# Probabilities placed by head pair, and the product with the values in three fp32r matmuls, in a four-layer kernel

## The chip, the cores and the metric

The kernel runs on one NeuronCore of a Trainium2 chip as one program. The metric is the device time of one execution in microseconds (us), taken as the median over several runs. The engines are TensorE (PE in the profile; PEld is its weight load), VectorE (DVE), ScalarE (ACT), GpSimd (POOL) and SyncE (SP), which here only issues DMAs. Each works through its own instructions in order, and they wait for one another on semaphores.

## The reference

x has shape 8 x 128 x 512. Three low-rank or selected linear layers are added to it one after the other, and then an attention layer, in which this change lies:

```python
q, k, v = x @ Wq.T, x @ Wk.T, x @ Wv.T            # 32 query heads, 8 key/value heads, D = 128
q, k = rope(rmsnorm(q, q_norm_w), pos), rope(rmsnorm(k, k_norm_w), pos)
k_all = concat([k_cache[block_table], k])          # 512 cached positions + 128 new ones
v_all = concat([v_cache[block_table], v])
scores = einsum("bqhd,bkhd->bhqk", q, repeat(k_all, 4)) * SCALE
scores = where(valid, scores, -1e30)
probs = softmax(scores)                            # per head 128 queries x 640 keys
o = einsum("bhqk,bkhd->bqhd", probs, repeat(v_all, 4))
x = x + o.reshape(8, 128, 4096) @ Wo.T
```

All data are 32-bit floats.

## The kernel before

**Stages.** The first 120 us do the first three layers. Then come 64 units, one for each pair of key/value head and batch entry: a unit is one key/value head with its group of four query heads (GROUP), over 640 keys in five chunks of 128 (CH = 5, of which CCH = 4 are cached).

**One unit.** TensorE projects queries, key and value from x_s, turns the cached keys and the rotated queries, and computes the scores of the four heads into ps_s. VectorE adds the mask and takes the minimum (`lowest`), ScalarE takes the exponential (`exps`), VectorE the reciprocal of its sum (`inverse`), ScalarE multiplies by it (`normalize`). For the product with the values the probabilities must have the keys on the partitions: VectorE transposes 32 x 32 blocks (`turn_blocks`, line 1152), and the blocks are brought to their places by two DMAs through memory: `place_blocks` writes `blocks` to `blocks_dram` in four DMAs (line 364), waits for them, and reads it back into `prob_t` (line 371). Then `values` on TensorE multiplies: for each of two pairs of heads five chunks, stationary operand `v_raw` (cached) or `v_new`, moving operand 256 columns of `prob_t`, both plain 32-bit floats, which the chip does in two passes per matmul (20 rows for ten matmuls in the trace). The result is split into a rounded part and a remainder (`out_high` on ScalarE, `out_low` on VectorE) and multiplied by the output weights (`put_out`).

**Split products.** All other large products run in fp32r, a 32-bit format with rounded operands. Both operands are split into a rounded part and a remainder, and `three` does three matmuls: high x high, high x low, low x high. The helpers are `copy` (line 638) on ScalarE, `rest` (line 1055) on VectorE, and `weight_low` (line 106) on GpSimd.

**Order.** It is written out by hand as one function `step(n)` for each engine, in loops over n. Step n does the scores and probabilities of unit n, the projections and turned keys of unit n+1, the values of unit n-1 and the output product of unit n-2. On TensorE the order is: scores of pair 0, queries, scores of pair 1, key and value, turned cached keys, `put_out`, turned queries, `values(n-1)`. On GpSimd it is: copy of the new value into `v_new`, gather of the next values by an indirect DMA (line 493), remainder of a chunk of weights (line 106), sum of the rotated queries (line 509), norm factors `rstd` (line 513), gather of the next keys. ScalarE needs `rstd` to scale the new key (line 659), and TensorE needs that scaled key and the summed queries before it turns them (lines 876 to 880).

**Buffers.** `ps_o1` holds the turned cached keys and then the values product of pair 1, which waits for `kc_lo_out`, the remainder of those keys. Weights come in chunks until unit 54; from unit 55 on neither VectorE nor GpSimd splits weights.

## Time and profile before

| | us |
|---|---|
| median of three runs | 1224.59 |
| lowest and highest | 1222.09, 1231.84 |
| the profiled execution | 1230.89 |
| its span, first to last instruction | 1229.2 |
| TensorE busy | 1139.0 (93%) |
| VectorE busy | 850.5 (69%) |
| ScalarE busy | 683.5 (56%) |
| GpSimd busy | 475.6 (39%) |
| mean granted clock of TensorE | 0.985 of full |

The busy time of an engine is its instructions' time on one execution; instructions overlap a little, so sums of durations are somewhat above it. In a timeline row the first number is the start, the second the time until the last instruction of the row ended, and the bracket the idle time of the engine before it with what released it. The rows below use line numbers of the kernel before.

### The profile page before, as it was taken

Reading aid. Unit: us, or ns where it says so; the run is one execution under the profiler, and the core shown is the slowest. Engines: PE = TensorE matmul, PEld = TensorE weight load, DVE = VectorE, ACT = ScalarE, POOL = GpSimd, SP = SyncE. Lnnn points to the kernel's source line nnn. Section 1 sums busy time; section 2 is a strip of 40 time slices with the busy share of each in tenths; the row PEclk is TensorE's granted clock in tenths of the full one; section 3 lists DMA queues with packets and bytes.
Section 4 is the critical chain, followed back from the end, with each engine's and each line's share of the span. In section 5 each row is a group of like instructions: output and inputs, shape, how many; then the busy total and the mean of one; then the engine's idle time right before and its main releaser. Section 6 shows DMA issues by size and latency. Waiting matters only on the chain.

```text
span 1229.2 us, 27100 instructions
## 1 busy us (share of the span) xinstructions
PE 1139.0 (93%) x6112; PEld 979.4 (80%) x6112; DVE 850.5 (69%) x2167; ACT 683.5 (56%) x1914; POOL 475.6 (39%) x570
## 2 busy tenths in 40 slices
PE   5998789999999999999999999999999999999986
PEld 3555678888888888888888888888888888888874
DVE  2335667777777777777777777776777777777671
ACT  2223556665565665565666565665656665566550
POOL 6752334444333343333444333343333443232310
PEclk8999799999999999999999999999999999999998
DMA  5573477777777787777777777787777777767764
GB/s 171 189 273 133 136 229 231 241 236 226 238 242 242 245 252 230 228 247 240 240 239 227 233 249 238 241 255 229 218 243 237 249 226 221 233 215 227 241 197 137
DMA packets 83690, 277.31 MB, mean 226 GB/s; under 512 B 12633, under 2 KB 12761, under 8 KB 74459
## 3 DMA queue, kind: packets, MB, share of 16 engines
q1 hardware_dynamic: 71368, 236.23, 61.3%
q0 software_dynamic: 11152, 36.72, 10.1%
q10 hardware_dynamic: 1154, 4.19, 0.9%
q8 instruction: 6, 0.10, 0.0%
q14 instruction: 10, 0.07, 0.0%
HBM read 186.92 MB, written 90.18 MB: 225 GB/s over the span
## 4 chain that ended last, share of the span: by engine, by line
PE 50%; DMA 30%; DVE 7%; issue 6%; SPq 5%; ACT 1%; DVEq 0%; POOL 0%; POOLq 0%; ACTq 0%
DMA blocks_placed<-blocks 15%; DMA prob_t<-blocks_placed 13%; PE ps_o L911 12%; PE ps_q L848 8%; SPq L364 4%; PE ps_kv L848 4%; DVE blocks L1152 3%; PE ps_s L748 3%; PE ps_s L750 3%; PE ps_s L749 3%; PE ps_x L750 2%; PE ps_x L748 2%; DVE kt_lo L1055 2%; PE ps_x L749 2%; PE ps_l L780 2%
## 5 line engine op out<-in xcount | busy, mean ns | idle before, releaser
L911 PE MATMUL ps_o<-prob_t,v_raw 128*128 128x256 f32 x1024 | 251.5, 390 | 57.9 <-DMA prob_t<-blocks_placed 53.6
L685 ACT ACTIVATE prob<-prob,low 128x640 f32<-128x640 f32 x256 | 210.1, 825 | 126.8 <-DVE low L1134 117.3
L911 PEld LDWEIGHTS ps_o<-prob_t,v_raw 128*128 128x128 f32 x1024 | 193.9, 194 | 90.5 <-issue 60.5
L1134 DVE CUSTOM_DVE_ANT_0 prob<-ps_s,mask,q_gain 128x640 f32<-128x640 f32 x256 | 215.7, 880 | 35.6 <-PE ps_s L750 35.6
L1152 DVE STREAM_TRANSPOSE blocks<-prob 128x640 f32<-128x640 f32 x256 | 214.0, 837 | 0.4 <-ACT prob L690 0.2
L690 ACT ACTIVATE prob<-prob,inv 128x640 f32<-128x640 f32 x256 | 196.7, 817 | 0.6 <-DVE inv L1140 0.6
L638 ACT ACTIVATE ot_hi<-ps_o 128x256 fp32r<-128x256 f32 x128 | 49.2, 384 | 241.3 <-PE ps_o L911 241.3
L748 PE MATMUL ps_s<-kt_hi,qt_hi 128*128 (+2 forms) x512 | 172.0, 336 | 5.2 <-DVE kt_lo L1055 3.7
L848 PE MATMUL ps_q<-w_hi,x_s 128*128 (+1 forms) x512 | 172.6, 397 | 0.0
L750 PE MATMUL ps_s<-kt_hi,qt_lo 128*128 (+2 forms) x512 | 160.3, 313 | 0.0
L749 PE MATMUL ps_s<-kt_lo,qt_hi 128*128 (+2 forms) x512 | 160.0, 313 | 0.0
L520 POOL COPY v_new<-v_next 128x128 f32 (+1 forms) x64 | 18.5, 289 | 343.5 <-PE ps_o L911 335.2
L106 POOL TENSOR_TENSOR w_lo<-w_raw,w_hi 128x640 f32 (+1 forms) x64 | 100.6, 1572 | 98.0 <-DVE w_hi L100 96.7
L1055 DVE TENSOR_TENSOR ot_lo<-ps_o,ot_hi 128x256 fp32r<-128x256 f32 x128 | 53.1, 415 | 123.2 <-ACT ot_hi L638 123.2
L509 POOL TENSOR_TENSOR rot<-rot_a,rot_b 128x512 f32<-128x512 f32 x64 | 83.2, 1301 | 90.1 <-DVE rot_b L1081 90.1
L848 PEld LDWEIGHTS ps_q<-w_hi,x_s 128*128 128x128 f32 x512 | 96.8, 189 | 21.1
L748 PE MATMUL ps_x<-w_hi,ot_hi 128*128 (+1 forms) x256 | 106.3, 415 | 2.0 <-DVE ot_lo L1055 2.0
L748 PEld LDWEIGHTS ps_s<-kt_hi,qt_hi 128*128 128x128 f32 x512 | 97.4, 190 | 10.7 <-DVE kt_lo L1055 4.3
L513 POOL TENSOR_TENSOR rstd<-var,neg_half 128x5 f32<-128x5 f32 x64 | 77.2, 1206 | 70.2 <-DVE var L1089 70.2
L848 PE MATMUL ps_q<-w_lo,x_s 128*128 (+1 forms) x256 | 101.6, 397 | 0.0
L749 PEld LDWEIGHTS ps_s<-kt_lo,qt_hi 128*128 128x128 f32 x512 | 97.5, 190 | 4.6
L848 PE MATMUL ps_kv<-w_hi,x_s 128*128 (+1 forms) x512 | 100.9, 281 | 0.0
(138 smaller groups left out, 2212.0 us busy)
## 6 DMA issues: line engine op xcount, KB each, us to landing
blocks_placed<-blocks SPq DMA_DIRECT2D x256, 320.0 KB
prob_t<-blocks_placed SPq DMA_DIRECT2D x64, 1280.0 KB
x_s<-xt_split SPq DMA_DIRECT2D x64, 512.0 KB
w_raw<-w_qkvo_dram SPq DMA_DIRECT2D x55, 320.0 KB
w<-w_t_dram SPq DMA_DIRECT2D x8, 1024.0 KB, 5.8
xt_split<-x3t ACTq DMA_DIRECT2D x8, 512.0 KB
w_raw<-w_qkvo_dram POOLq DMA_DIRECT2D x9, 320.0 KB, 5.7
xbt<-x_t_dram SPq DMA_DIRECT2D x8, 256.0 KB, 2.7
```

The costliest lines, as they stand in the source:

```text
L106: return nc.gpsimd.tensor_tensor(lo, raw, hi.bitcast(F32), ALU.subtract)
L509: nc.gpsimd.tensor_tensor(rot[:, 0:GROUP, :], rot_a[:, 0:GROUP, :], rot_b[:, 0:GROUP, :], ALU.add).then_inc(q_summed, 1)
L685: nc.scalar.activation(prob[:, h, :], prob[:, h, :], ACT.Exp, bias=low[:, h:h + 1], scale=-1.0, accum_out=total[:, h:h + 1]).then_inc(exp_ ...
L690: nc.scalar.activation(prob[:, h, :], prob[:, h, :], ACT.Copy, scale=inv[:, h:h + 1]).then_inc(prob_done, 1)
L748: nc.tensor.matmul(dst, lh, rh, start=first, stop=False)
L749: nc.tensor.matmul(dst, lh, rl, start=False, stop=False)
L750: return nc.tensor.matmul(dst, ll, rh, start=False, stop=final)
L848: mm = nc.tensor.matmul(dst, x_s[:, int(i % 3 == 2), k * P:(k + 1) * P], w_rest if i % 3 == 1 else w, start=i == 0, stop=i == 3 * KT - 1)
L911: mm = nc.tensor.matmul(ps_o[pair][:, 0:PAIR], v, turned_probs(c, pair), start=c == 0, stop=c == CH - 1)
L1055: return nc.vector.tensor_tensor(dst, src, high.bitcast(F32), ALU.subtract)
L1134: nc.vector.tensor_tensor_reduce(out=prob[:, h, :], in0=ps_s[:, score_slot(h):score_slot(h) + KEYS], in1=mask[:, :], scale=q_gain[:, h:h + ...
L1152: nc.vector.transpose(blocks[:, :, :, h, :].rearrange("p j c q -> p c j q"), prob[:, h, :].rearrange("p (c j k) -> p c j k", c=CH, j=NB)). ...
```

## The change

The placing of the probabilities is cut in two: `place_blocks(n, pair)` writes and reads back one pair of heads, with its own part of `blocks_dram`, `prob_t` and semaphores, and starts as soon as that pair is turned. A unit then has eight writes, each of 32 x 4 pieces of 1280 bytes (before, four with pieces of 2560 bytes), and two reads of 640 KB.

The product with the values goes through `three`. For this both operands are split. The values: VectorE rounds the 640 columns of `v_raw` (which now holds the new value too) into `v_hi` (`values_high`), GpSimd takes the remainder `v_lo` (`values_low`). The probabilities: ScalarE rounds each pair, 1280 columns, into `pt_hi` (`probs_high`), and VectorE and GpSimd each subtract over half of the columns (640), in place in `prob_t` (`probs_low_first`, `probs_low_rest`). `values` waits for both halves of each pair. Since `v_raw` is free once it is split, the gather of the next values waits for `v_split`, and it is issued one unit earlier.

```diff
-        blocks_dram = nc.dram_tensor("blocks_placed", [NB, BLOCK, NB, CH * GROUP * BLOCK], F32).ap()
+        blocks_dram = nc.dram_tensor("blocks_placed", [2, NB, BLOCK, NB, RUN], F32).ap()
...
-            v_new = sb("v_new", [P, D], scope=p2)
             prob = sb("prob", [P, GROUP, KEYS], scope=p2)
-            blocks = sb("blocks", [P, NB, CH, GROUP, BLOCK], scope=p2)
-            prob_t = sb("prob_t", [P, NB * CH * GROUP * BLOCK], scope=p2)
+            blocks = sb("blocks", [P, 2, NB, CH, GROUP // 2, BLOCK], scope=p2)
+            prob_t = sb("prob_t", [P, 2, NB * RUN], F32R, scope=p2)
+            pt_hi = sb("pt_hi", [P, 2, NB * RUN], F32R, scope=p2)
+            v_hi = sb("v_hi", [P, CH * D], F32R, scope=p2)
+            v_lo = sb("v_lo", [P, CH * D], F32R, scope=p2)
...
+            CUT = NB // 2 * RUN
...
-                    def place_blocks(n, first=False):
-
-                        sp.wait_ge(blocks_turned, GROUP * (n + 1))
+                    def place_blocks(n, pair, first=False):
+
+                        sp.wait_ge(blocks_turned, GROUP * n + 2 * pair + 2)
                         sp.nop(nofuse=True)
                         if not first:
-                            sp.wait_ge(pt_in, 16 * n)
+                            sp.wait_ge(pt_in[pair], 16 * n)
                             sp.nop(nofuse=True)
                         for a in range(NB):
-                            sp.dma_start(blocks_dram[:, :, a, :].rearrange("j i r -> i j r"),
-                                         blocks[a * BLOCK:(a + 1) * BLOCK, :, :, :, :].rearrange("p j c h q -> p j (c h q)")).then_inc(blocks_out, 16)
-                        sp.wait_ge(blocks_out, 16 * NB * (n + 1))
+                            sp.dma_start(blocks_dram[pair, :, :, a, :].rearrange("j i r -> i j r"),
+                                         blocks[a * BLOCK:(a + 1) * BLOCK, pair, :, :, :, :].rearrange("p j c h q -> p j (c h q)")).then_inc(blocks_out[pair], 16)
+                        sp.wait_ge(blocks_out[pair], 16 * NB * (n + 1))
                         sp.nop(nofuse=True)
                         if not first:
-                            sp.wait_ge(pv_done, 2 * n)
+                            sp.wait_ge(pv_done, 2 * (n - 1) + pair + 1)
                             sp.nop(nofuse=True)
-                        sp.dma_start(prob_t[:, :], blocks_dram.rearrange("j i a r -> (j i) (a r)")).then_inc(pt_in, 16)
+                        sp.dma_start(prob_t[:, pair, :].bitcast(F32), blocks_dram[pair].rearrange("j i a r -> (j i) (a r)")).then_inc(pt_in[pair], 16)
...
-                        place_blocks(n, first)
+                        place_blocks(n, 0, first)
+                        place_blocks(n, 1, first)
...
-                        pool.wait_ge(pv_done, 2 * u)
+                        pool.wait_ge(v_split, u)
...
-                    def move_new_value(u, values):
+                    def move_new_value(u, first=False):
+                        if not first:
+                            pool.wait_ge(v_split, u)
+                            pool.nop(nofuse=True)
                         pool.wait_ge(vn_out, u + 1)
-                        if values:
-                            pool.wait_ge(pv_done, 2 * u)
                         pool.nop(nofuse=True)
-                        nc.gpsimd.tensor_copy(v_new[:, :], next_value(u)).then_inc(vn_moved, 1)
-
-                    def step(n, weights, keys, last, first=False, second=False):
-
-                        if not first:
-                            move_new_value(n - 1, not second)
-                            if not second:
-                                next_values(n - 1)
+                        nc.gpsimd.tensor_copy(v_raw[:, CCH * D:], next_value(u)).then_inc(vn_moved, 1)
+
+                    def values_low(u):
+                        pool.wait_ge(v_hi_out, u + 1)
+                        nc.gpsimd.tensor_tensor(v_lo[:, :], v_raw[:, :], v_hi[:, :].bitcast(F32), ALU.subtract).then_inc(v_split, 1)
+
+                    def probs_low_rest(u, pair):
+                        pool.wait_ge(pt_hi_out, 2 * u + pair + 1)
+                        nc.gpsimd.tensor_tensor(prob_t[:, pair, CUT:], prob_t[:, pair, CUT:].bitcast(F32),
+                                                pt_hi[:, pair, CUT:].bitcast(F32), ALU.subtract).then_inc(pt_lo_rest, 1)
+
+                    def step(n, weights, keys, last, first=False):
+
+                        if not first:
+                            values_low(n - 1)
+                        move_new_value(n, first)
+                        if not first:
+                            next_values(n)
                         if weights:
                             pool.wait_ge(w_rounded, n + AHEAD + 1)
                             weight_low(n + AHEAD, w_raw[:, 0, :]).then_inc(w_split, 1)
+                        if not first:
+                            probs_low_rest(n - 1, 0)
                         if not last:
                             sum_queries(n + 1)
                             norm_factors(n + 1)
+                        if not first:
+                            probs_low_rest(n - 1, 1)
...
+                    def probs_high(u, pair):
+                        act.wait_ge(pt_in[pair], 16 * (u + 1))
+                        copy(pt_hi[:, pair, :], prob_t[:, pair, :].bitcast(F32)).then_inc(pt_hi_out, 1)
+
                     def step(n, last, head=True, out=True, first=False):
                         if head:
                             out_high(n - 2, 1, first=first)
                         exps(n, 0)
                         exps(n, 1)
+                        if out:
+                            probs_high(n - 1, 0)
                         normalize(n, 0)
...
+                            probs_high(n - 1, 1)
                         normalize(n, 2)
...
-                        pe.wait_ge(v_in, 16 * (u + 1))
-                        pe.wait_ge(vn_moved, u + 1)
-                        pe.wait_ge(pt_in, 16 * (u + 1))
+                        pe.wait_ge(v_split, u + 1)
                         if not first:
                             pe.wait_ge(ot_lo_out, 2 * u)
                         for pair in (0, 1):
+                            pe.wait_ge(pt_lo_first, 2 * u + pair + 1)
+                            pe.wait_ge(pt_lo_rest, 2 * u + pair + 1)
                             if pair == 1:
                                 pe.wait_ge(kc_lo_out, cached)
                             for c in range(CH):
-                                v = v_raw[:, c * D:(c + 1) * D] if c < CCH else v_new[:, :]
-                                mm = nc.tensor.matmul(ps_o[pair][:, 0:PAIR], v, turned_probs(c, pair),
-                                                      start=c == 0, stop=c == CH - 1)
+                                cut = slice(c * D, (c + 1) * D)
+                                mm = three(ps_o[pair][:, 0:PAIR], (v_hi[:, cut], v_lo[:, cut]),
+                                           (turned_probs(pt_hi, c, pair), turned_probs(prob_t, c, pair)), c == 0, c == CH - 1)
                             mm.then_inc(pv_done, 1)
...
+                    def values_high(u, first=False):
+                        dve.wait_ge(v_in, 16 * (u + 1))
+                        dve.wait_ge(vn_moved, u + 1)
+                        dve.wait_ge(xt_stored, 16 * B) if first else dve.wait_ge(pv_done, 2 * u)
+                        nc.vector.tensor_copy(v_hi[:, :], v_raw[:, :]).then_inc(v_hi_out, 1)
+
+                    def probs_low_first(u, pair):
+                        dve.wait_ge(pt_hi_out, 2 * u + pair + 1)
+                        rest(prob_t[:, pair, 0:CUT], prob_t[:, pair, 0:CUT].bitcast(F32), pt_hi[:, pair, 0:CUT]).then_inc(pt_lo_first, 1)
...
+                        if out:
+                            values_high(n - 1, first=not head)
                         dve.wait_ge(mask_set, n + 1)
...
                         turn_blocks(n, 1)
+                        if out:
+                            probs_low_first(n - 1, 0)
                         inverse(n, 2)
...
                             cached_low(n + 1, ps_o1)
-                        turn_blocks(n, 2)
+                        if out:
+                            probs_low_first(n - 1, 1)
+                        turn_blocks(n, 2, first)
```

On GpSimd the next-to-last step (unit 62, written out without the loop's register rows; in the loop the remainder of the weights, `w_lo`, stands between the gather and `rot`) reads before:

```order
L520 COPY v_new<-v_next 128x128
L490 COPY v_row<-row_id 128x1
L493 DMA v_raw<-v_rows_dram,v_row 128x512
L509 TENSOR_TENSOR rot<-rot_a,rot_b 128x512
L513 TENSOR_TENSOR rstd<-var,neg_half 128x5
```

and now:

```order
L533 TENSOR_TENSOR v_lo<-v_raw,v_hi 128x640
L529 COPY v_raw<-v_next 128x128
L498 COPY v_row<-row_id 128x1
L501 DMA v_raw<-v_rows_dram,v_row 128x512
L537 TENSOR_TENSOR prob_t<-prob_t,pt_hi 128x640
L517 TENSOR_TENSOR rot<-rot_a,rot_b 128x512
L521 TENSOR_TENSOR rstd<-var,neg_half 128x5
L537 TENSOR_TENSOR prob_t<-prob_t,pt_hi 128x640
```

Two remainders stand ahead of the norm factors `rstd` that did not stand there, and one behind them.

On ScalarE, in the loop, from the scaling of the new key to the rounding of the turned queries and key, before:

```order
L659 ACTIVATE rot<-key_sum,rstd 128x128
L638 ISA
L638 ACTIVATE kt_hi<-ps_o 128x512
L690 ACTIVATE prob<-prob,inv 128x640 x2
L638 ACTIVATE qt_hi<-ps_q 128x512
L638 ISA
L638 ACTIVATE kt_hi<-ps_kv 128x128
```

and now:

```order
L682 ACTIVATE rot<-key_sum,rstd 128x128
L661 ISA
L661 ACTIVATE kt_hi<-ps_o 128x512
L661 ACTIVATE pt_hi<-prob_t 128x1280
L713 ACTIVATE prob<-prob,inv 128x640 x2
L661 ACTIVATE qt_hi<-ps_q 128x512
L661 ISA
L661 ACTIVATE kt_hi<-ps_kv 128x128
```

The rounding of pair 1 stands behind the cached keys and ahead of the last two normalizations.

On VectorE, in the loop, from the remainder of the cached keys to the last transposed head, before:

```order
L1055 TENSOR_TENSOR kt_lo<-ps_o,kt_hi 128x512
L1152 STREAM_TRANSPOSE blocks<-prob 128x5x4x32
L1055 TENSOR_TENSOR qt_lo<-ps_q,qt_hi 128x512
L1055 ISA
L1055 TENSOR_TENSOR kt_lo<-ps_kv,kt_hi 128x128
L1106 TENSOR_SCALAR q_gain<-rstd 128x4
L1152 STREAM_TRANSPOSE blocks<-prob 128x5x4x32
```

and now (line 1088 is `rest`):

```order
L1088 TENSOR_TENSOR kt_lo<-ps_o,kt_hi 128x512
L1187 REGISTER_ALU
L1088 TENSOR_TENSOR prob_t<-prob_t,pt_hi 128x640
L1195 STREAM_TRANSPOSE blocks<-prob 128x5x4x32
L1088 TENSOR_TENSOR qt_lo<-ps_q,qt_hi 128x512
L1088 ISA
L1088 TENSOR_TENSOR kt_lo<-ps_kv,kt_hi 128x128
L1139 TENSOR_SCALAR q_gain<-rstd 128x4
L1195 STREAM_TRANSPOSE blocks<-prob 128x5x4x32
```

VectorE's half of pair 1 stands ahead of the third transposed head.

## Rows read from the trace of the kernel before

**Rows 1.** The page's first part: busy time, share of the span, instructions

```profile
PE 1139.0 (93%) x6112; PEld 979.4 (80%) x6112; DVE 850.5 (69%) x2167; ACT 683.5 (56%) x1914; POOL 475.6 (39%) x570
```

**Rows 2.** Waits, grouped: us in total, times, longest

```profile
PE ps_o L911 <- DMA prob_t<-blocks_placed: 53.6, 32, 3.1
```

**Rows 3.** Timeline of PE, 610 to 646 us: start, us, what [idle before <-releaser]

```profile
611.12 1.97 PE L911 MATMUL ps_o<-prob_t,v_raw 128*128 128x256 f32 x8 [1.57 <-DMA prob_t<-blocks_placed]
...
627.03 1.89 PE L911 MATMUL ps_o<-prob_t,v_raw 128*128 128x256 f32 x8
...
631.16 0.47 PE L748 MATMUL ps_s<-kt_hi,qt_hi 128*128 x1
...
644.69 1.53 PE L911 MATMUL ps_o<-prob_t,v_raw 128*128 128x256 f32 x6 [1.64 <-DMA prob_t<-blocks_placed]
```

**Rows 4.** The chain that ended last, 600 to 680 us: start, us, what

```profile
622.02 1.42 PE ps_kv L848 x12
...
632.58 6.19 DMA blocks_placed<-blocks
638.96 5.46 DMA prob_t<-blocks_placed
```

**Rows 5.** Timeline of DVE, 628 to 646 us

```profile
629.66 0.83 DVE L1152 STREAM_TRANSPOSE blocks<-prob 128x640 f32<-128x640 f32 x1
...
631.96 0.42 DVE L1055 TENSOR_TENSOR ot_lo<-ps_o,ot_hi 128x256 fp32r<-128x256 f32 x1 [0.77 <-ACT ot_hi L638]
...
634.52 0.49 DVE L100 CAST w_hi<-w_raw 128x640 f32 x1
...
643.34 0.68 DVE L1055 TENSOR_TENSOR kt_lo<-ps_o,kt_hi 128x512 f32 x1
```

**Rows 6.** Timeline of SyncE's queue, 628 to 662 us

```profile
630.70 3.45 SPq L364 DMA_DIRECT2D blocks_placed<-blocks  x4
```

**Rows 7.** Timeline of POOL, 631 to 645 us, one step

```profile
631.80 0.29 POOL L520 COPY v_new<-v_next 128x128 f32 x1 [4.26 <-PE ps_o L911]
632.04 0.18 POOL L490 COPY v_row<-row_id 128x1 int32 x1
633.00 0.97 POOL L493 DMA_INDIRECT v_raw<-v_rows_dram,v_row  x1 [0.77 <-POOL v_row L490]
635.56 1.58 POOL L106 TENSOR_TENSOR w_lo<-w_raw,w_hi 128x640 f32 x1 [1.59 <-DVE w_hi L100]
637.84 1.30 POOL L509 TENSOR_TENSOR rot<-rot_a,rot_b 128x512 f32<-128x512 f32 x1 [0.70 <-DVE rot_b L1081]
640.21 1.21 POOL L513 TENSOR_TENSOR rstd<-var,neg_half 128x5 f32<-128x5 f32 x1 [1.07 <-DVE var L1089]
```

**Rows 8.** Timeline of ACT, the same step

```profile
631.55 0.38 ACT L638 ACTIVATE ot_hi<-ps_o 128x256 fp32r<-128x256 f32 x1 [1.77 <-PE ps_o L911]
...
635.48 1.54 ACT L690 ACTIVATE prob<-prob,inv 128x640 f32<-128x640 f32 x2
...
641.51 0.41 ACT L659 ACTIVATE rot<-key_sum,rstd 128x128 f32<-128x128 f32 x1
641.82 0.58 ACT L638 ACTIVATE kt_hi<-ps_o 128x512 f32 x1
```

**Rows 9.** Timeline of POOL and DVE in the first stage, 62 to 90 us

```profile
63.70 0.69 DVE L970 TENSOR_TENSOR xbt_lo<-xbt,xbt_hi 128x512 fp32r<-128x512 f32 x1 [4.89 <-ACT xbt_hi L555]
...
86.87 1.53 POOL L106 TENSOR_TENSOR w_lo<-w_raw,w_hi 128x640 fp32r<-128x640 f32 x1
...
87.29 1.67 DVE L970 TENSOR_TENSOR xbt_lo<-xbt,xbt_hi 128x512 fp32r<-128x512 f32 x1 [4.89 <-ACT xbt_hi L555]
```

**Rows 10.** Timeline of PE, 838 to 858 us

```profile
845.90 2.65 PE L911 MATMUL ps_o<-prob_t,v_raw 128*128 128x256 f32 x8 [1.92 <-DMA prob_t<-blocks_placed]
```

**Rows 11.** Windows: busy time of each engine, PE's granted clock, DMA share

```profile
848.00:850.00 2.00, 2.00 (x6) 1.58 (x5) 0.15 (x1) 0.39 (x1) 0.00 (x0) 0.50 0.83 181
```

**Rows 12.** Timeline of PE at the end

```profile
1215.70 3.65 PE L911 MATMUL ps_o<-prob_t,v_raw 128*128 128x256 f32 x8 [4.27 <-DMA v_raw<-v_rows_dram,v_row]
```

35 lines of the change are left out of this document (22 added, 13 removed).

## The prediction

> **What bounds the kernel now.** First the share of the engines: TensorE is busy 93% of the span [rows 1]. That suggests a TensorE bound, but the waits show the one thing it still waits for in the steady state: in 32 units, every second one, the values product waits for the probabilities to come back from memory, 53.6 us in all [rows 2]. TensorE's timeline shows the rhythm: the product starts at 611.12, 627.03 and 644.69 [rows 3]. One unit takes 15.91 us without the wait, the next 17.66 with it, so two take 33.57 and one 16.79. The chain over the same stretch tells which loop that is [rows 4]: the last head of unit n is turned (629.66 plus 0.83, so 630.49 [rows 5]), SyncE issues four writes (630.70, 3.45 us [rows 6]), they have landed by 638.77, the read is issued at 638.96 and takes 5.46, and TensorE starts at 644.69 [rows 3, 4]. From the turned head to the product it is 14.2 us, and the product of the unit before stands ahead of the scores from which the next probabilities are made. So the kernel runs on a loop over two units, with pure TensorE work (15.9 a unit) close under it.
>
> **TensorE's part.** A unit has 20 passes of 256 columns; those up to 631.16 began at 627.03, so they take 4.13 us, or 0.21 each [rows 3]. An fp32r matmul of 256 columns takes 0.118: 12 of them 1.42 [rows 4]. The change makes 30, that is 3.55 us. TensorE's work falls by 0.6 to 15.3 a unit. The moving operand keeps its pattern of runs of 32 columns; fp32r with such runs is not in the trace. The value taken is 0.118, from the same number of columns; the other end is the 0.21 of the plain passes with the same runs, which would make 6.2 us and 2.7 more a unit.
>
> **The placing.** By pair, the leg from the last turned head to its data shrinks. Before: 8.3 to the landed writes, 0.2, 5.7 to TensorE [rows 3 to 6]. A pair has as many write pieces as the whole had, of half the size, and half the read. If issuing sets the pace (3.45 for the same count of pieces) and a tail of about 2 stays, a write takes 5.6 and a read about 3.8, 9.5 together. The upper bound is that nothing shrinks: 14.2 for each pair. Pair 0 starts after the second head. From its end to the last head's, VectorE has two more heads of 0.83, three operations on 512 columns of about 0.68 and some small ones, some 4.2 us by [rows 5], and now two halves of 0.8 in between. The last head is turned 0.7 before the product ends (630.49 against 631.16 [rows 3, 5]), now up to a microsecond later, so pair 1's data is there 9 to 10 us into the next step. ScalarE comes to it after the cached keys, 11 us in (641.82 against 631.16 [rows 3, 8]). Pair 0's data comes some 6 us before pair 1's, 3 to 4 us in, and ScalarE comes to it after two exponentials, 4.3 us in (635.48 [rows 8]). So the placing is hidden, by about 1 us for either pair. This loop is gone as the bound, and the question is what is late next.
>
> **What is late next: GpSimd.** The order gives GpSimd three more subtractions of 640 columns per step, each as long as the one of weights, 1.58 us [rows 7], 4.7 us together. In the gaps of 39% busy [rows 1] they would fit. But they lie in one chain that closes over a single unit, because rounding the values has to wait for the product of the unit before (it overwrites what that reads), and GpSimd's norm factors stand behind everything it does with values, weights and pair 0. I follow it from the last matmul of the product through one step, with the row for each piece:
>
> - ScalarE's `ot_hi` starts 0.05 later, VectorE's `ot_lo` 0.41 after it [rows 5, 8], `v_hi` 0.35 after that and takes 0.49, as the cast of 640 columns does [rows 5]. Sum 1.30.
> - GpSimd, 0.1 later: `v_lo` 1.58, 0.1, the new value 0.24, from the row copy to the gather 0.96, the gather 0.97, weights 1.58, pair 0's remainder 1.58, `rot` 1.30, `rstd` 1.21 [rows 7]. Sum 10.92. In the row of before `rstd` was done at 641.42, 9.9 after the product, since it had idle time ahead of each piece.
> - ScalarE: 0.09, the new key 0.31 (641.51 to 641.82), the cached keys 0.58 less 0.1 of overlap [rows 8], then rounding pair 1. Its price: from 256 to 512 columns 0.38 becomes 0.58, so 768 more cost 0.6, in all 1.2; two operations of 640 take 1.54 [rows 8]. I take 1.25. Sum 13.05.
> - GpSimd's half of pair 1: 0.05, 1.58, 0.1. Sum 14.78.
> - TensorE: 15 matmuls 1.77, and 0.16 until the last has ended. **Sum 16.71 us.**
>
> That is already the 16.79 of before. Two places can only add.
>
> **The two halves of a remainder** wait for the same `pt_hi`, and both engines are free by then (VectorE's `cached_low` ends as the rounding does). VectorE's half costs 0.81: 0.42 for 256 columns, 0.68 for 512 [rows 5]. Whether the two run beside each other is the disputed cost. The rows of the first stage show the same pair of instructions meeting: GpSimd subtracts from 86.87 to 88.40, VectorE's subtraction of two SBUF operands starts at 87.29 and takes 1.67 instead of 0.69 (63.70), that is until 0.56 after GpSimd's end [rows 9]. So one waits for the other. Whoever is first, the pair of halves takes 2.13 (GpSimd first) to 2.33 (VectorE first), not 1.58: plus 0.55 to 0.75. I take 0.75: VectorE starts 0.41 after ScalarE does [rows 5, 8], that is at once, GpSimd some 0.1 later. The other place is the copies of `v_hi` and of the weights on VectorE, which fall beside GpSimd's small copies: 0 to 0.5, I take 0.3.
>
> The Trainium skill says the same in "SBUF — State Buffer", section "SBUF: two separate sides": VectorE and GpSimd share one port pair under an exclusive lock, taken also by a VectorE instruction with two SBUF inputs against a GpSimd one that reads SBUF. By this rule splitting a remainder between the two engines is little better than doing the halves in turn; the trace agrees in the one meeting above, and without the lock the sum would stay at 16.71.
>
> So a step takes 16.71 + 0.75 + 0.3 = 17.76 us, 0.97 more than before. **Steps without weights** (the last eight or so) lose 1.58 on GpSimd: about 16.2, 0.6 less than before. **At the end** the product waited for the gather of the values (4.27 us, until 1215.70 [rows 12]), which is now issued a unit earlier, and the last leg shrinks from 14.2 + 4.1 to about 9.5 + 1.25 + 2.3 + 1.8: some 4 less, I take 5 with the gather. Sum: 53 x 0.97 - 8 x 0.6 - 5 = +42 us.
>
> The profiled execution took 1230.89, so it would be 1273. The median of before is 0.5% under its profiled execution: **1267 us**.
>
> **What hides the rest.** ScalarE's rounding of pair 0 (1.25) stands ahead of two normalizations; the squares behind them wait for VectorE's rotation (line 1081) and leave idle time, and behind the squares `rstd` is later than ScalarE in any case, so I count nothing; without that cover it would be 1.25 a step. VectorE gets 2.1 us more; 69% busy [rows 1] of 16.79 is 11.6, so at least 13.7 of 17.8. Its last turned head moves some 2 us later, which the placing can bear. If the GpSimd chain were shorter, TensorE would be next: 15.3 and, as an estimate, 0.5 of waits for the rounding of pair 1, 15.8.
>
> **Rivals.**
>
> *The halves run side by side* and the small copies cost nothing: 16.71 a step, 53 x -0.08 - 5 - 5 = -14, profiled 1217, so 1211 to 1225. For it: only one such meeting is shown. Against: that one [rows 9]. 13%.
>
> *Faster: the GpSimd chain doesn't close*, because its instructions overlap or the values part is finished before TensorE asks, and the two gains show: no wait on the placing, 0.6 less on TensorE. The next bound is 15.8 a step: 61 x -1.0 = -60, so 1165. It decides by the length of GpSimd's part: a gain of over 1% needs a step under 16.6, 1.2 less than my sum, so each of the three new subtractions would have to cost 0.4 less, or `rstd` to be done 9.7 us after the product. In the rows GpSimd's instructions follow each other without overlap [rows 7]. 10%.
>
> *The placing is the bound*: a write by pair takes as long as before. SyncE blocks on each: 2 x (8.3 + 0.3) + 0.9 for the two other issues is 18.1 us a step, and pair 0 comes too late for ScalarE. Then 18.2 to 18.7 a step, 61 x 1.65 = +100, so 1325. For it: the count of pieces is the same for half the bytes, and the issue alone is 3.45. Against: half the bytes. 12%.
>
> *TensorE's clock.* With the forecast it idles twice per step, about 1 us before the turned queries and 2 us before pair 1. In the steady part of before a single wait of 1.92 us [rows 10] was followed by a stretch at a granted clock of 0.50, which is the level of 1.2 GHz [rows 11], while those of 1.57 and 1.64 [rows 3] were not. Both matmul groups behind the waits are on the loop; if it fell in every second unit for 3.4 us, it would cost 0.9 a unit more: 1315. 10%.
>
> **How the numbers follow.** My forecast, 1250 to 1290, has 55%. The range of 8 in 10 leaves out the fast rival and the worst of the slow ones: 1212 to 1328. A measurement of this kernel can tell about 1% from no change. Faster by over 1% (under 1212): the fast rival and a part of the first, 14%. Within 1%: the rest of the first and the low edge of the forecast, 14%. Slower: 72%.
>
> **What would show it.** In the profile after: `rstd` some 10.9 us after the end of the values product, with GpSimd without idle time from `v_lo` to it; TensorE waiting for the scaled key before the turned queries (about 1 us) and for `pt_lo_rest` before pair 1 (1.5 to 2 us), in every unit and no longer in every second; the wait on `prob_t` gone from TensorE and not on ScalarE; one of the two halves of pair 1 at 1.4 us or more (VectorE) or 2.3 (GpSimd); fp32r passes 0.118 apart. Wrong would be: ScalarE's `pt_hi` waiting for a DMA, `pt_lo` halves overlapping at 0.81 and 1.58, or a clock under 0.95.

## The result, and the profile after

The changed kernel takes 1278.44 us, the median of four runs (1278.27 to 1279.61), the kernel before 1228.21 beside it: a ratio of 1.0415, 95% interval 1.0361 to 1.0469. **It is 4.2% slower.** The profiled execution took 1278.57 us, its span is 1276.9.

The page of the changed kernel, the parts on busy time and on the chain that ended last:

```profile
PE 1103.5 (86%) x6752; PEld 961.1 (75%) x6752; DVE 1045.5 (82%) x2359; ACT 816.8 (64%) x2042; POOL 813.0 (64%) x762
...
POOL 32%; PE 29%; issue 19%; DVE 8%; ACT 5%; POOLq 3%; DMA 2%; DVEq 1%; SPq 0%; ACTq 0%
```

Against [rows 1], TensorE has lost 35 us of busy time in spite of 640 more matmuls, and GpSimd has gained 337. The second line is the finding. In the kernel before it begins with PE 50% and DMA 30%. Now DMA has 2%, and GpSimd, the engine with the lowest busy share beside ScalarE, leads with 32%. An engine that is busy 64% of the time can be the bound if the rest is waiting inside its own loop.

The waits of the changed kernel, grouped (us in total, times, longest):

```profile
POOL prob_t L537 <- ACT pt_hi L661: 147.6, 66, 4.6
...
POOL v_lo L533 <- DVE v_hi L1184: 106.0, 63, 4.5
...
PE ps_o L781 <- issue: 80.5, 58, 4.3
...
ACT rot L682 <- POOL rstd L521: 78.4, 59, 1.9
PE ps_q L912 <- ACT rot L682: 56.4, 57, 2.3
```

The wait of TensorE for `prob_t` from memory [rows 2] isn't there any more. In its place stand five that hang together and come in nearly every unit. They form a loop: `v_hi`, `v_lo`, ..., `rstd`, `rot`, `pt_hi`, `prob_t`, the product.

One step on TensorE's timeline (the second pair's product starts at 601.98 and at 619.73, 17.75 us apart; in nearly all units with weights it is 17.7 to 17.8):

```profile
601.98 0.36 PE L781 MATMUL ps_o<-pt_hi,v_hi 128*128 128x256 f32 x1 [1.37 <-issue]
602.17 0.28 PE L782 MATMUL ps_o<-prob_t,v_hi 128*128 128x256 f32 x1
602.29 0.28 PE L783 MATMUL ps_o<-pt_hi,v_lo 128*128 128x256 f32 x1
...
615.87 0.63 PE L912 MATMUL ps_q<-ident,rot 128*128 128x128 f32 x4 [0.92 <-ACT rot L682]
...
619.73 0.36 PE L781 MATMUL ps_o<-pt_hi,v_hi 128*128 128x256 f32 x1 [1.36 <-issue]
```

GpSimd's timeline between the two:

```profile
605.35 1.57 POOL L533 TENSOR_TENSOR v_lo<-v_raw,v_hi 128x640 fp32r<-128x640 f32 x1 [1.51 <-DVE v_hi L1184]
607.33 0.29 POOL L529 COPY v_raw<-v_next 128x128 f32 x1 [0.40 <-POOL v_lo L533]
...
608.54 0.99 POOL L501 DMA_INDIRECT v_raw<-v_rows_dram,v_row  x1 [0.77 <-POOL v_row L498]
609.54 1.59 POOL L107 TENSOR_TENSOR w_lo<-w_raw,w_hi 128x640 f32 x1
611.07 1.58 POOL L537 TENSOR_TENSOR prob_t<-prob_t,pt_hi 128x640 fp32r<-128x640 f32 x1
612.59 1.31 POOL L517 TENSOR_TENSOR rot<-rot_a,rot_b 128x512 f32<-128x512 f32 x1
614.02 1.21 POOL L521 TENSOR_TENSOR rstd<-var,neg_half 128x5 f32<-128x5 f32 x1
617.45 2.18 POOL L537 TENSOR_TENSOR prob_t<-prob_t,pt_hi 128x640 fp32r<-128x640 f32 x1 [2.22 <-ACT pt_hi L661]
```

ScalarE's in the same step:

```profile
604.02 0.39 ACT L661 ACTIVATE ot_hi<-ps_o 128x256 fp32r<-128x256 f32 x1 [2.04 <-PE ps_o L783]
...
615.32 0.40 ACT L682 ACTIVATE rot<-key_sum,rstd 128x128 f32<-128x128 f32 x1 [1.40 <-POOL rstd L521]
615.63 0.58 ACT L661 ACTIVATE kt_hi<-ps_o 128x512 f32 x1
616.11 1.26 ACT L661 ACTIVATE pt_hi<-prob_t 128x1280 fp32r<-128x1280 f32 x1
```

And VectorE's:

```profile
604.78 0.48 DVE L1184 CAST v_hi<-v_raw 128x640 fp32r<-128x640 f32 x1
...
612.41 1.53 DVE L1122 TENSOR_SCALAR var<-sq 128x5 f32<-128x5 f32 x1
...
617.41 0.81 DVE L1088 TENSOR_TENSOR prob_t<-prob_t,pt_hi 128x640 fp32r<-128x640 f32 x1
```

Read in order of time this is the chain: product ends, `ot_hi` 604.02, `v_hi` 604.78, `v_lo` 605.35, every piece on GpSimd close behind the one before until 615.23, `rot` 615.32, `pt_hi` 616.11 to 617.37, GpSimd's half 617.45 to 619.63, product 619.73. In [rows 7] GpSimd waits 1.59, 0.70 and 1.07 us ahead of three of these pieces. Here those waits are gone. The last half takes 2.18 us instead of 1.58, because VectorE began its own half 0.04 earlier.

SyncE's queue in the same step:

```profile
612.04 0.35 SPq L356 DMA_DIRECT2D x_s<-xt_split  x1
612.72 0.34 SPq L361 DMA_DIRECT2D w_raw<-w_qkvo_dram  x1
615.67 1.83 SPq L371 DMA_DIRECT2D blocks_placed<-blocks  x4
619.92 0.34 SPq L378 DMA_DIRECT2D prob_t<-blocks_placed  x1
621.33 2.33 SPq L371 DMA_DIRECT2D blocks_placed<-blocks  x4
626.98 0.34 SPq L378 DMA_DIRECT2D prob_t<-blocks_placed  x1
```

Four writes are issued and have landed 4.25 us later for pair 0 and 5.65 for pair 1. For all heads at once it was 8.3 [rows 4, 6].

### The profile page after: what moved, and what is told of

It reads as the page before. It is cut to its first block, busy times and chain, and to the rows that moved or that the text cites. A ratio compares the mean times of both kernels' runs of the same rounds, so it can differ in the third digit from the quotient of the medians.

```text
span 1276.9 us, 30220 instructions
## 1 busy us (share of the span) xinstructions
PE 1103.5 (86%) x6752; PEld 961.1 (75%) x6752; DVE 1045.5 (82%) x2359; ACT 816.8 (64%) x2042; POOL 813.0 (64%) x762
## 4 chain that ended last, share of the span: by engine, by line
POOL 32%; PE 29%; issue 19%; DVE 8%; ACT 5%; POOLq 3%; DMA 2%; DVEq 1%; SPq 0%; ACTq 0%
POOL v_lo L533 7%; POOL w_lo L107 7%; POOL prob_t L537 7%; PE ps_o L781 6%; POOL rot L517 6%; POOL rstd L521 5%; PE ps_o L783 5%; PE ps_o L782 5%; PE ps_q L912 3%; PE ps_l L813 2%; DVE v_hi L1184 2%; ACT rot L682 2%; ACT ot_hi L661 2%; DVE blocks L1195 1%; DVE prob_t L1088 1%
## 5 line engine op out<-in xcount | busy, mean ns | idle before, releaser
L537 POOL TENSOR_TENSOR prob_t<-prob_t,pt_hi 128x640 fp32r<-128x640 f32 x128 | 237.8, 1858 | 147.8 <-ACT pt_hi L661 147.6
L781 PE MATMUL ps_o<-pt_hi,v_hi 128*128 128x256 f32 x640 | 191.5, 299 | 91.6 <-issue 80.5
L781 PEld LDWEIGHTS ps_o<-pt_hi,v_hi 128*128 128x128 f32 x640 | 121.0, 189 | 104.1 <-issue 95.7
L782 PE MATMUL ps_o<-prob_t,v_hi 128*128 128x256 f32 x640 | 181.7, 284 | 0.0
L783 PE MATMUL ps_o<-pt_hi,v_lo 128*128 128x256 f32 x640 | 181.2, 283 | 0.0
L533 POOL TENSOR_TENSOR v_lo<-v_raw,v_hi 128x640 fp32r<-128x640 f32 x64 | 100.9, 1577 | 106.0 <-DVE v_hi L1184 106.0
L661 ACT ACTIVATE pt_hi<-prob_t 128x1280 fp32r<-128x1280 f32 x128 | 161.3, 1260 | 10.3 <-DMA prob_t<-blocks_placed 10.3
L782 PEld LDWEIGHTS ps_o<-prob_t,v_hi 128*128 128x128 f32 x640 | 121.4, 190 | 0.0
L783 PEld LDWEIGHTS ps_o<-pt_hi,v_lo 128*128 128x128 f32 x640 | 121.1, 189 | 0.0
L1088 DVE TENSOR_TENSOR prob_t<-prob_t,pt_hi 128x640 fp32r<-128x640 f32 x128 | 109.5, 856 | 7.0 <-ACT pt_hi L661 7.0
```

The source lines that it names most:

```text
L533: nc.gpsimd.tensor_tensor(v_lo[:, :], v_raw[:, :], v_hi[:, :].bitcast(F32), ALU.subtract).then_inc(v_split, 1)
L537: nc.gpsimd.tensor_tensor(prob_t[:, pair, CUT:], prob_t[:, pair, CUT:].bitcast(F32), pt_hi[:, pair, CUT:].bitcast(F32), ALU.subtract).then ...
L661: return nc.scalar.activation(dst, src, ACT.Copy)
L781: nc.tensor.matmul(dst, lh, rh, start=first, stop=False)
L782: nc.tensor.matmul(dst, lh, rl, start=False, stop=False)
L783: return nc.tensor.matmul(dst, ll, rh, start=False, stop=final)
```

## The experiments

All times are medians, with the ratio to the kernel before, run on the same chip, and its 95% interval. "Step" is the mean distance between the first score operations (`low`) of two units on VectorE, units 8 to 52, when weights are still loaded. "Writes" is the mean time on SyncE from the first of four writes to the read behind them, for pair 0 and pair 1, between 200 and 1050 us. Runs 4, 6 and 7 leave work or bytes out and compute something else; they only show what a part costs.

| kernel | us | ratio | step | writes |
|---|---|---|---|---|
| before | 1224.7 to 1228.2 | 1 | 16.79 | 7.8, all heads |
| after | 1278.44 | 1.0415 | 17.79 | 4.25, 6.00 |
| 1 placing by pair alone | 1256.99 | 1.0292 (1.0225 to 1.0358) | 17.32 | 8.05, 6.28 |
| 2 pair 0's half late | 1219.85 | 0.9962 (0.9933 to 0.9992) | 16.70 | 4.56, 5.16 |
| 3 pair 1 on VectorE | 1258.47 | 1.0297 (1.0240 to 1.0353) | 17.44 | 5.81, 6.20 |
| 4 no remainders | 1239.52 | 1.0137 (1.0083 to 1.0192) | 17.07 | 6.03, 6.17 |
| 5 pair 0 on VectorE | 1220.14 | 0.9962 (0.9928 to 0.9997) | 16.71 | 4.51, 5.12 |
| 6 = 4, keys behind | 1199.73 | 0.9813 (0.9776 to 0.9850) | 16.31 | 5.04, 6.30 |
| 7 = 1, short inputs | 1162.89 | 0.9502 (0.9477 to 0.9528) | 15.86 | 5.65, 6.80 |
| 8 one placing | 1810.99 | 1.4794 (1.4752 to 1.4836) | 26.05 | 7.8, all heads |
| 9 = 1, ScalarE loads | 1213.76 | 0.9907 (0.9876 to 0.9937) | 16.62 | 7.18, 6.81 |
| 10 = before, ScalarE loads | 1233.25 | 1.0068 (1.0041 to 1.0095) | 16.84 | 7.7, all heads |
| 11 = 5, ScalarE loads | 1250.56 | 1.0217 (1.0171 to 1.0263) | 17.26 | 5.46, 5.70 |
| 12 = after, ScalarE loads | 1326.21 | 1.0820 (1.0778 to 1.0862) | 18.71 | 5.13, 6.55 |

### 1. Only the placing by pair

The kernel before with the placing of the changed one; the product stays f32.

```diff
-                        place_blocks(n, first)
+                        place_blocks(n, 0, first)
+                        place_blocks(n, 1, first)
```

> The kernel before with the placing by head pair alone; the product with the values stays in plain 32-bit floats, and nothing is split. Theory (the loop over two units through the placing was the bound before, and the pairs break it): the wait of 1.6 to 1.7 us in every second unit goes, and a unit takes TensorE's own 15.9 us instead of 16.8: some 54 us less, a ratio to before of 0.956, about 1175 us. Rival (SyncE, blocked on two writes in turn, takes the place of the loop, or the next wait is close behind): ratio 0.99 to 1.01.

Slower, 1.0292. The theory, that the placing is hidden once it is done by pair, failed. SyncE's queue in this kernel:

```profile
614.70 0.35 SPq L350 DMA_DIRECT2D x_s<-xt_split  x1
615.37 0.34 SPq L355 DMA_DIRECT2D w_raw<-w_qkvo_dram  x1
616.03 3.08 SPq L365 DMA_DIRECT2D blocks_placed<-blocks  x4
624.89 0.34 SPq L372 DMA_DIRECT2D prob_t<-blocks_placed  x1
625.46 2.26 SPq L365 DMA_DIRECT2D blocks_placed<-blocks  x4
631.25 0.34 SPq L372 DMA_DIRECT2D prob_t<-blocks_placed  x1
632.25 0.35 SPq L350 DMA_DIRECT2D x_s<-xt_split  x1
```

The loop over two units through the turned heads is indeed gone (SyncE waits for turned blocks 3.6 us in all), but it is replaced by SyncE's own round: issue the inputs, write, wait, read, write, wait, read, 17.55 us from `x_s` to `x_s`. SyncE waits 586.5 us for writes to land, and pair 0's writes, of half the bytes, take as long as those of the whole had (8.05 against 7.8).

### 2. GpSimd's half of pair 0 behind the norm factors

```diff
-                        if not first:
-                            probs_low_rest(n - 1, 0)
                         if not last:
                             sum_queries(n + 1)
                             norm_factors(n + 1)
                         if not first:
+                            probs_low_rest(n - 1, 0)
                             probs_low_rest(n - 1, 1)
```

> The changed kernel with one instruction moved: GpSimd's half of pair 0's remainder stands behind the norm factors instead of ahead of the sum of the queries. Theory (one chain through GpSimd closes over each step, and this piece of 1.58 us lies on it): a step falls from 17.75 us to VectorE's bound, seen in the steps without weights, of about 16.7: 53 x 1.05 = 56 us less, about 1222 us, ratio to before 0.995. Rival (the bound is the load of VectorE or the count of instructions of GpSimd, not their order): within 5 us of 1278, ratio 1.04.

As the theory had it. The same work in another order gives 1219.85 us, 58 less than the changed kernel, so the chain through `rstd` was the bound. In this kernel TensorE's one wait is for VectorE's half (0.84 and 0.21 us), and VectorE is busy 754 of the 800 us from 200 to 1000.

### 3. Pair 1's remainder wholly on VectorE

```diff
-                        if not first:
-                            probs_low_rest(n - 1, 1)
```

VectorE's subtraction goes over 1280 columns for pair 1.

> The changed kernel with the whole remainder of pair 1 on VectorE, 1280 columns in one instruction, and none of it on GpSimd; pair 0 as it is. Theory (the two halves exclude each other, so that the pair of them takes 2.25 us from the rounding): one instruction takes 1.49 us, a step 0.75 less, 53 x 0.75 = 40 us less, about 1239, ratio 1.009. Rival (the halves run side by side and the 2.19 us of GpSimd's half have another cause): 1.49 instead of 1.58, 5 us less, ratio 1.037. A second rival: VectorE is so full that its longer instruction gives back more than half: ratio 1.025 or more.

A miss for the theory: 1.0297, the step fell by only 0.35. It is the second rival, a full VectorE. The loop through GpSimd is still the one that closes. One turn of it:

```profile
604.70 1.48 DVE L1086 TENSOR_TENSOR prob_t<-prob_t,pt_hi 128x1280 fp32r<-128x1280 f32 x1
610.05 1.58 POOL L533 TENSOR_TENSOR v_lo<-v_raw,v_hi 128x640 fp32r<-128x640 f32 x1 [5.55 <-DVE v_hi L1182]
620.04 0.40 ACT L679 ACTIVATE rot<-key_sum,rstd 128x128 f32<-128x128 f32 x1 [0.60 <-POOL rstd L521]
```

From the end of the rounding to the end of the subtraction it is 1.53 us, 0.73 less than the 2.26 of the two halves. But VectorE then works without a gap from 604.70 until the end of `v_hi` at 609.96, and comes to `v_hi` later: 1.69 us from the product to its end instead of 1.28. From there to the end of `rstd` it is 9.99, ScalarE takes 2.13 and TensorE 2.09, in sum 17.43. The 5.55 us ahead of `v_lo` are GpSimd's wait for `v_hi`; they don't take it out of the loop. ScalarE's `pt_hi` also waits for the read now, 77.7 us in all, in 62 units. SyncE is not the bound: it waits for turned heads 160.1 us in all.

### 4. No remainders of the probabilities

```diff
-                            pe.wait_ge(pt_lo_first, 2 * u + pair + 1)
-                            pe.wait_ge(pt_lo_rest, 2 * u + pair + 1)
+                            pe.wait_ge(pt_hi_out, 2 * u + pair + 1)
```

The four subtractions of a unit are left out as well.

> The changed kernel without the four subtractions that take the remainder of the probabilities: the placed probabilities themselves are multiplied where the remainder was. Rounding, splitting of the values, placing and all 30 matmuls stay. Theory: the chain loses 1.58 for pair 0 and 2.25 for pair 1, and a step comes to TensorE's 15.3 plus some waits, 15.6: about 130 us less than the changed kernel, 1148 us, ratio 0.935. Rival (the values' part or the placing is a bound of its own): a step stays above 16.4, ratio 0.98 or more.

Again a miss: with all four halves gone, 1239.52 us. SyncE's queue:

```profile
614.38 0.34 SPq L361 DMA_DIRECT2D w_raw<-w_qkvo_dram  x1
617.01 2.39 SPq L371 DMA_DIRECT2D blocks_placed<-blocks  x4
623.30 0.34 SPq L378 DMA_DIRECT2D prob_t<-blocks_placed  x1
```

and ScalarE's rounding of the pair of the unit before:

```profile
610.79 1.27 ACT L655 ACTIVATE pt_hi<-prob_t 128x1280 fp32r<-128x1280 f32 x1 [1.80 <-DMA prob_t<-blocks_placed]
```

Pair 0's writes take 6.29 us, against 4.25 in the changed kernel, with the same bytes and pieces. Here a second loop has become the bound, and it isn't SyncE's queue, which waits for turned heads 134.1 us in all, in nearly every unit ahead of pair 0's writes (the 2.29 us between 614.72 and 617.01). It goes through the data of pair 0: writes, read, rounding (`pt_hi` waits for the read in 59 units, 85.2 us), normalizations, turned head, writes of the next unit, 17.07 us in the mean. Two things could stretch the writes. GpSimd's key gather is issued at 617.45 here, 0.4 us after them (at 620.54 in the changed kernel, when they have landed), and the transfers of `x_s` and `w_raw` are issued shortly ahead. Run 6 takes the first away here; run 7 takes the second away in run 1's kernel.

### 5. Pair 0's remainder wholly on VectorE

With no half of pair 0 left on GpSimd, this is the changed kernel with one assignment changed: VectorE subtracts over all 1280 columns of pair 0. Against run 2:

```diff
-                            probs_low_rest(n - 1, 0)
                             probs_low_rest(n - 1, 1)
```

> The kernel with GpSimd's half of pair 0 behind the norm factors, and that half now given to VectorE: VectorE subtracts the whole 128x1280 of pair 0, pair 1 stays in halves. Theory (two engines that meet over the same stretch gain nothing): in the kernel that it starts from VectorE's half of pair 0 lasts 2.06 us, because GpSimd's 1.55 us half is in its way, and TensorE waits 0.84 us for it; the whole remainder alone on VectorE should take about 1.5 us (cached_low does 512 columns from PSUM in 0.68, a half of 640 takes 0.8 when undisturbed), so the step falls from 16.7 to about 16.1 us and the time to 1190 (0.970 of the kernel before the change). Rival: the placing through SyncE is already nearly the bound (it set 17.3 us a step in the two runs whose VectorE or GpSimd was relieved), so a key gather that is issued earlier stretches pair 0's writes and the time stays at 1220 or rises to 1245.

The same time as run 2, so the theory's further 30 us didn't come. VectorE's timeline says why:

```profile
604.92 1.45 DVE L1086 TENSOR_TENSOR prob_t<-prob_t,pt_hi 128x1280 fp32r<-128x1280 f32 x1
607.61 1.61 DVE L1086 TENSOR_TENSOR prob_t<-prob_t,pt_hi 128x640 fp32r<-128x640 f32 x1
```

Pair 0 takes the 1.45 us expected, but now pair 1's half meets GpSimd's (606.97 to 608.54) and takes 1.61 instead of 1.01. In run 2 the two took 2.06 + 1.01 = 3.07 us of VectorE's time, here 1.45 + 1.61 = 3.06. The stall moved and didn't shrink. The rival named the number (1220), but its reason was wrong, since the writes took 4.51 us and TensorE waited for VectorE alone.

### 6. Run 4, with the key gather behind pair 0's writes

```diff
                         if keys:
+                            pool.wait_ge(blocks_out[0], 16 * NB * (n + 1))
                             next_keys(n + 2)
```

> The kernel without remainders of the probabilities (the placed probabilities themselves are multiplied where the remainder stood, so the sum is another), and GpSimd's gather of the cached keys now waits until pair 0's writes have landed. Theory (the key gather is in the writes' way): there the gather is issued 0.4 us after pair 0's writes and these take 6.3 us, against 4.25 to 4.5 us in the two kernels whose gather comes later; moved behind them the writes fall to about 4.5 us, the step from 17.4 to about 16.0 us, and the time from 1239.5 to about 1170 (0.955). Rival (the writes are slow because SyncE issues them within 2.6 us of the two input transfers, whoever gathers what): writes stay at 6 us or more, the step at 17.3 us, the time at 1235 to 1245 (1.01).

The writes of pair 0 fell from 6.03 to 5.04 us and the step from 17.07 to 16.31, so the gather's place does cost here. It is a good half of what the theory asked.

### 7. Run 1, with short input transfers

```diff
-                        sp.dma_start(x_s[:, :, :].bitcast(F32), xt_dram[bass.ds(u & 7, 1), :, :, :].rearrange("a p s c -> p (a s) c")).then_inc(x_s_in, 16)
+                        sp.dma_start(x_s[:, :, 0:64].bitcast(F32), xt_dram[bass.ds(u & 7, 1), :, :, 0:64].rearrange("a p s c -> p (a s) c")).then_inc(x_s_in, 16)
```

and `w_raw` the same.

> The kernel before the change with the placing by pair alone, and SyncE's transfers of the next input and weights cut from 512 and 320 KB to an eighth and a tenth (the rest of the tiles keeps old numbers, so the output is another). Theory (pair 0's writes stand in line behind these 832 KB, which SyncE issues 0.7 to 1.3 us ahead of them): pair 0's writes fall from 8.2 to 8.9 us to about 6 us, the step from 17.4 to about 16.0 us or to what TensorE's own work takes, and the time from 1257 to about 1175 to 1190 (0.965). Rival (the writes are limited by their own 1280-byte pieces and the gathers): pair 0's writes stay above 7.5 us, the time above 1240.

Better than the theory's number: 1162.89 us, and every step from the third unit on is 15.8 to 16.0 us. The window of the steady part, with each engine's busy time, PE's granted clock, DMA share and GB/s:

```profile
200.00:1000.00 800.00, 800.00 (x4487) 717.17 (x4486) 632.60 (x1663) 513.09 (x1458) 334.84 (x403) 1.00 0.68 205
```

TensorE is busy 800 us of 800. This is what [rows 3] called the 15.9 of pure TensorE work, and it is the floor of this kernel with the f32 product. Pair 0's writes fell from 8.05 to 5.65 us.

### 8. The changed kernel with one placing per unit

```diff
-                        place_blocks(n, 0, first)
-                        place_blocks(n, 1, first)
+                        place_blocks(n, first)
```

> The changed kernel with one placing per unit again, as before the change (2560-byte pieces, one read of 1280 KB), the three matmuls, the rounding and the halves all kept and in the same order. Theory (the new order of the engines needs pair 0's probabilities early): ScalarE rounds pair 0 some 4 us after the last head of the unit before has been turned, while the whole placing lands about 10 us after it, so ScalarE waits 5 to 6 us for it at every step, with everything behind it; the step grows to about 20 us or more and the time to 1380 to 1450 (1.15). Rival (GpSimd's chain alone sets 17.75 us and the wait lies in its shadow): the time stays at 1278 (1.04) or falls, since the wide pieces are written faster.

The sign as expected and the size far beyond: 1810.99, a step of 26.05 us. From its waits:

```profile
ACT pt_hi L663 <- DMA prob_t<-blocks_placed: 591.7, 64, 10.2
```

That is 9.2 us a unit, and it lies on the path, since ScalarE normalizes the next heads only behind `pt_hi`, and the next placing needs those. The step is 8.3 us longer. A part may be the clock, which the theory had left out: between 200 and 1000 us TensorE is busy 529.90 of 800 us and its mean granted clock is 0.83 of full, against 1.00 in the changed kernel. How much of the step that is, no run here shows apart. The two parts of the change can't be taken apart in this order: the product as written needs the placing by pair.

### 9 to 12. The input transfers issued by ScalarE

In four kernels `x_s` and `w_raw`, whole again, are issued by ScalarE: `x_s` behind the new value, `w_raw` between the scaled key and the cached keys.

```diff
+                        if weights:
+                            next_weights(n + 1)
                         if not last:
                             cached_high(n + 1, ps_o1, first=not out)
```

Run 9 is run 1 with it:

> The kernel before the change with the placing by pair alone, and the transfers of the next input and the next weights, whole again, issued by ScalarE on its own queue instead of by SyncE. Theory (pair 0's writes stand in line behind these 832 KB on SyncE's queue, and SyncE, which waits for each landing, is the loop): pair 0's writes fall from 8.2 to 8.9 us to 5.5 to 6.5 us, and SyncE saves the 1.3 us of two issues, so the step falls from 17.4 to 15.9 to 16.3 us and the time from 1257 to about 1165 to 1190 (0.96 of the kernel before). Rival (the transfers share the same DMA engines from whichever queue, and it is their bytes that cost): pair 0's writes stay at 7.5 us or more, SyncE gains only its issue time, and the time is 1225 to 1250 (1.01).

1213.76 us, between the two. Pair 0's writes fell by 0.9 us only, pair 1's rose by 0.5. SyncE also saves 1.3 us of issuing, and the step fell by 0.70; SyncE now waits for turned heads again, 73.9 us in all. So of the 2.4 us by which run 7 shortened pair 0's writes, most came from fewer bytes, not from a free queue, while of the 1.46 us of its step about half comes with all bytes kept. The Trainium skill has the rule in "DMA: Bandwidth & Descriptors", section "Issuing engines are not separate DMA queues": whoever issues, the transfers run on the same 16 DMA engines, and issuing from several saves the issue time only. Writes of 7.18 us against 5.65 agree with it.

Run 10 is the kernel before with it:

> The kernel before the change, unchanged but for the transfers of the next input and the next weights, which ScalarE issues. Theory (in the kernel before, SyncE waits for turned blocks after it has issued them, so they have landed before the writes start and nothing stands in line): the writes keep their 5.6 us, the loop of two units its 33.6 us, and the time is 1225 within 1% (1.00). Rival (the gain of the run with short inputs was simply fewer bytes in the chip, or a freer SyncE, and comes with any placing): 1195 or less (0.975).

As the theory had it, within 1%.

Run 11 is run 5 with it:

> The changed kernel with pair 0's remainder wholly on VectorE, and the two input transfers issued by ScalarE. Theory (there VectorE is the bound, TensorE waits for it alone, 0.25 and 0.79 us a step, and the writes, 4.4 us, are off the path): the time stays at 1220 (0.996 of the kernel before). Rival (the placing still holds a part of that step): 1195 (0.975).

Run 12 is the changed kernel with it:

> The changed kernel, unchanged but for the two input transfers, which ScalarE issues. Theory (GpSimd's chain closes over one step at 17.75 us and the placing lies in its shadow): the step stays at 17.7 to 17.8 us and the time at 1278 (1.042 of the kernel before). Rival (pair 1's placing, which ScalarE waits for in a few steps, or the key gather still sets part of the step): 1265 or less (1.03).

Both missed, and on the slow side. I hadn't counted that ScalarE's issue of `w_raw` stands between `rot` and `kt_hi`. In the changed kernel `kt_hi` begins 0.31 us after `rot`; in run 12 it is 0.84 (617.81 and 618.65). ScalarE is 64% busy, but these 0.53 us lie on the loop, and where the loop runs undisturbed the step is 18.3 us, 0.55 more than 17.75. The rest, up to the mean of 18.71, goes with the clock. TensorE's two waits in one unit of run 12, ahead of the turned queries and of pair 1's product:

```profile
806.12 0.63 PE L930 MATMUL ps_q<-ident,rot 128*128 128x128 f32 x4 [0.93 <-ACT rot L682]
810.53 0.36 PE L799 MATMUL ps_o<-pt_hi,v_hi 128*128 128x256 f32 x1 [1.88 <-issue]
```

and the window behind them (the clock is the third number from the end):

```profile
812.00:816.00 4.00, 4.00 (x20) 3.96 (x19) 2.06 (x5) 0.38 (x1) 1.95 (x2) 0.60 0.91 276
```

Behind waits of 0.93 and 1.88 us the granted clock fell to 0.60 of full in this window (a mixture of 2.4 and 1.2 GHz), and over 200 to 1000 us it was 0.96. The step that follows took 18.81 us. In the changed kernel the same two waits are 0.92 and 1.36 us, and the clock was 1.00. So run 12 shows what the rival on TensorE's clock had described, and the changed kernel doesn't.

In run 11 the same issue stands there (`kt_hi` begins 0.68 us after `rot`), but the loop is VectorE's. Its half of pair 1 now begins at 603.32, 0.09 us behind GpSimd's, and takes 2.15 us instead of the 1.61 of run 5, where it began 0.64 behind. That is the 0.55 us by which the step grew (16.71 to 17.26).

## Why the prediction was right, and where it was not

The sign, the mechanism and the step were right: 17.76 us forecast, 17.75 read. Not every term was.

| from the last product, us | forecast | after |
|---|---|---|
| to the end of `v_hi` | 1.30 | 1.28 |
| GpSimd to the end of `rstd` | 9.62 | 9.97 |
| ScalarE to the end of `pt_hi` | 2.13 | 2.14 |
| the two halves | 2.38 | 2.26 |
| TensorE, with 0.1 to its start | 2.03 | 2.10 |
| copies beside copies | 0.30 | 0 |
| sum | 17.76 | 17.75 |

- **GpSimd's part** lacked 0.35: 0.30 of it is the new value's copy, which begins 0.40 after `v_lo` and not 0.1.
- **The halves** do exclude each other, with VectorE first, as forecast. The pair took 2.26 and not 2.38.
- **The 0.3 for the copies** of `v_hi` and of the weights wasn't there (0.48 and 0.49, as alone). That the sum is right to 0.01 is luck. Its terms are right to 0.35.
- **fp32r** passes are 0.118 apart with runs of 32 columns as without, and TensorE does less work, as forecast. It buys nothing, since TensorE waits.
- **The placing is hidden** came true in the changed kernel (ScalarE waits for it 10.3 us in all). But the prediction gave it as a property of the placing by pair, and run 1 shows that it isn't: alone it makes the kernel 2.9% slower. The missing step is SyncE's round. With two placings it waits for two landings per unit, and the writes are issued beside 832 KB of inputs and a gather. I had priced that round at 18.1 us for the rival "the placing is the bound", and gave that rival 12%; in run 1 it closes at 17.3. In the changed kernel SyncE's queue has room, since it waits 203.8 us for turned heads. Nearer is the rival's other half, pair 0's data coming too late for ScalarE: that loop closes at 17.07 in run 4, with writes of 6.03 us. How near it is in the changed kernel, where the writes take 4.25, no run shows.
- **What comes next, if GpSimd's chain were shorter**, was wrong. I named TensorE at 15.8 us a step. Runs 2 and 5 stop at 16.7, with VectorE busy 754 and 756 of 800 us. I had VectorE's load too small: 69% is its share of the whole span, and 11.6 us a step was worked out from it, but between 200 and 1000 us it is busy 601.56 of 800 us in the kernel before, which is 12.6 a step, and 754.36 in run 2, which is 15.7, with its stalls behind GpSimd. Run 3 shows it too: there VectorE's queue makes `v_hi` 0.41 us later. Behind VectorE stands pair 0's placing (run 4). The fast rival at 1165 us was therefore not to be had by the route that it named: even without any remainder, run 4 took 1239.52.
- **Steps without weights** were forecast at 16.2 and are 16.87 in the mean of the last eight. GpSimd's chain does get shorter there, but VectorE's half of pair 1 takes its place: it now begins behind GpSimd's (which starts at 1114.47), lasts 1.94 us instead of 0.81, and TensorE waits for it 1.08 us at 1116.77.

```profile
1114.77 1.94 DVE L1088 TENSOR_TENSOR prob_t<-prob_t,pt_hi 128x640 fp32r<-128x640 f32 x1
1116.77 0.39 PE L781 MATMUL ps_o<-pt_hi,v_hi 128*128 128x256 f32 x1 [1.08 <-DVE prob_t L1088]
```

- **The end** was to give 5 us and gave none. The last unit's product, pair 0 and then pair 1, still waits 3.00 and 4.29 us:

```profile
1257.60 0.36 PE L781 MATMUL ps_o<-pt_hi,v_hi 128*128 128x256 f32 x1 [3.00 <-POOL prob_t L537]
1264.29 0.55 PE L781 MATMUL ps_o<-pt_hi,v_hi 128*128 128x256 f32 x1 [4.29 <-issue]
```

The span grew by 47.7 us where the sum had 42. The distance from the first unit's scores to the last one's grew by 48.1, and what lies around it shrank by 0.4. The end gave 4.6 less than forecast, the eight steps without weights some 3 less (before: 17.07), and the steps with weights cost 2 less. The other half of the 11 us by which the median missed is that the profiled execution of before lay 0.5% above its median, and that of the changed kernel didn't.

**Where the 4.2% come from.** Taking pair 0's half out of the chain, by moving it (run 2) or giving it to VectorE (run 5), brings the whole loss back and 0.4% more. What stays open is why the gain of the placing and of TensorE together is so small there. Runs 2 and 5 show VectorE as the bound. That a kernel with less on VectorE would reach 15.8 wasn't shown: run 4 has less on it and is held by pair 0's placing, and run 6, which relieves this too, stands at 16.31. Of run 7's gain I can't say how much is a queue and how much bandwidth beyond what run 9 tells.

Three versions that do the whole work lie under both kernels: runs 2 and 5 at 0.996, hardly apart from no change, and **run 9 at 0.991** (0.9876 to 0.9937), the placing by pair with the f32 product kept and the input transfers issued by ScalarE. It isn't at the floor of run 7: four of its steps are 19 to 21 us long. Before one of them TensorE waits 2.83 us for `prob_t`, and the product behind it runs at half the clock. From run 9, TensorE's timeline:

```profile
588.78 3.54 PE L931 MATMUL ps_o<-prob_t,v_raw 128*128 128x256 f32 x8 [2.83 <-DMA prob_t<-blocks_placed]
```

and a window of it:

```profile
590.00:592.00 2.00, 2.00 (x7) 1.55 (x6) 0.00 (x0) 0.00 (x0) 0.00 (x0) 0.52 0.05 19
```

## What to carry to other kernels

Before work is handed to an engine with a low busy share, follow what the new piece stands ahead of, from the end of one unit's bottleneck operation to the same point a unit later: here an engine at 39% took three pieces of 1.6 us and became the bound, and moving one of them behind `rstd` gave back all of it. Work that must wait for the previous unit's product turns a pipeline of two units into a loop over one, and then every piece on it counts, a 0.4 us DMA issue included. A transfer cut in two costs an issuing engine that waits for it two landings. Try such a part alone, because a second bound can hide right under the first. And take an engine's load from the steady part, not from its share of the whole span.
